# Attention's running totals: from one VectorE addition a unit to an identity product on TensorE and two copies on ScalarE

## The reference, cut to what matters

```python
h = (x @ W.T).reshape(n, H, D)                      # H = 8 heads of D = 32
alpha = einsum(h[src], a_src) + einsum(h[dst], a_dst)
enc = relu(edge_attr @ edge_W.T + edge_b).reshape(-1, H, D)
alpha = alpha + sum(enc * h[dst], axis=-1)
alpha = where(alpha >= 0, alpha, 0.2 * alpha)
amax = segment_max(alpha, dst)
ex = exp(alpha - amax[dst])
denom = segment_sum(ex, dst)
attn = ex / maximum(denom[dst], 1e-10)
out = segment_sum(h[src] * attn[..., None], dst)
```

## Time and profile before

| | us |
|---|---|
| median of 3 runs | 2576.47 |
| lowest, highest | 2573.31, 2578.95 |
| the profiled execution's own time | 2573.98 |
| its span, first to last instruction | 2572.2 |
| attention, first to last instruction (1429.5 to 2113.4) | 683.9 |
| of it, first group's sums to group 100's (1478.5 to 2079.2) | 600.7 |

### The profile page before, as it was taken

How to read it: one execution, slowest core, us unless ns; L and a number is a source line. 1 busy time by engine, 2 the same in 40 slices (tenths; PEclk the granted TensorE clock), 3 DMA queues, 4 the chain that set the end, 5 groups by cost and what they waited for, 6 DMA issues and landing times. The chain is left out here.

```text
span 2572.2 us, 42829 instructions
## 1 busy us (share of the span) xinstructions
PE 1882.3 (73%) x12059; PEld 1450.7 (56%) x12059; DVE 1646.2 (64%) x3381; ACT 839.1 (33%) x2217; POOL 1187.9 (46%) x1128
## 2 busy tenths in 40 slices
PE   3266666654299974799927777777777867978997
PEld 1245454543177753699925455555555642328997
DVE  7565656553187777665567499999999987022222
ACT  7333333322000011233316344444444433423332
POOL 0277777777400000355500577777777710004442
PEclk9687878777599996899968899999999998988999
DMA  3265555444588824222251455555555515101111
GB/s 81 77 202 186 197 179 179 169 165 164 185 296 292 294 104 151 91 71 73 69 173 37 147 148 145 142 146 145 147 144 144 144 56 211 37 1 50 51 53 30
DMA packets 198893, 345.71 MB, mean 134 GB/s; under 512 B 63569, under 2 KB 114738, under 8 KB 198287
## 3 DMA queue, kind: packets, MB, share of 16 engines
q1 hardware_dynamic: 145306, 196.20, 23.3%
q0 software_dynamic: 53088, 146.77, 19.0%
q10 hardware_dynamic: 274, 0.00, 0.0%
HBM read 222.74 MB, written 121.04 MB: 134 GB/s over the span
## 5 line engine op out<-in xcount | busy, mean ns | idle before, releaser
L1967 POOL DMA_INDIRECT att_rows<-hdram,top_ix x440 | 507.6, 1154 | 265.6 <-issue 133.2
L861 POOL DMA_INDIRECT mtab<-first_w,msgs_ix x280 | 276.7, 988 | 85.4 <-issue 80.8
L1163 POOL IOTA route_column<- 128x50 f32 (+1 forms) x2 | 0.3, 169 | 548.1 <-ACTq L1159 548.1
L1398 PE MATMUL exp_y<-exp_own,exp_ht 128*128 128x256 f32 x1032 | 239.0, 380 | 2.4 <-issue 2.4
L2048 PE MATMUL att_p_acc<-att_msg,att_hot 128*128 128x264 f32 x880 | 224.1, 399 | 21.1 <-DVE att_total L2220 13.3
L729 PE MATMUL msgs_p_m<-nodes_n,msgs_hott 128*128 x592 | 184.8, 466 | 46.3 <-issue 27.6
L2082 ACT ACTIVATE att_enc<-att_p_z 128x1024 f32<-128x1024 f32 x110 | 112.6, 1023 | 298.2 <-PE att_p_z L1988 298.2
L1398 PEld LDWEIGHTS exp_y<-exp_own,exp_ht 128*128 128x128 f32 x1032 | 188.7, 190 | 24.6 <-issue 3.1
L2048 PEld LDWEIGHTS att_p_acc<-att_msg,att_hot 128*128 128x128 f32 x880 | 161.8, 194 | 59.6 <-issue 32.7
L861 POOL DMA_INDIRECT mtab<-msgs_rw,msgs_ix x160 | 159.6, 998 | 69.8 <-issue 45.1
L627 DVE TENSOR_TENSOR first_w<-msgs_p_m,msgs_sorted 128x1024 f32<-128x1024 f32 x70 | 85.6, 1223 | 141.9 <-PE msgs_p_m L729 116.5
(11 more groups left out here) (403 smaller groups left out, 4003.0 us busy)
## 6 DMA issues: line engine op xcount, KB each, us to landing
first_w<-mtab SPq DMA_DIRECT2D x77, 520.0 KB, 4.6
etab<-msgs_et SPq DMA_DIRECT2D x110, 288.0 KB, 2.5
att_hz<-etab SPq DMA_DIRECT2D x110, 288.0 KB, 2.9
msgs_rw<-mtab SPq DMA_DIRECT2D x45, 520.0 KB, 4.7
first_w<-in_L_ffn_w SPq DMA_DIRECT2D x16, 512.0 KB, 4.6
ffn0x_w<-in_L_ffn_w SPq DMA_DIRECT2D x16, 512.0 KB
ffn_w<-in_L_ffn_Wd SPq DMA_DIRECT2D x8, 1024.0 KB, 10.7
att_rows<-hdram,top_ix POOLq DMA_INDIRECT x440
```

What stands on the lines that cost most here:

```text
L861: nc.gpsimd.indirect_dma_start(mtab, bass.IndirectOffsetOnAxis(ap=ix[:, g, q:q + 1], axis=0), rw[g % RS][:, q, :], None).then_inc(s_free[g ...
L1398: last = T.matmul(y[t % 2][:, 0:C], ht[t % 2][:, f, :], own2[:, f, :], start=(f == 0), stop=(f == FC - 1))
L1967: nc.gpsimd.indirect_dma_start(rows[:, g % RS, q, :], None, hdram, bass.IndirectOffsetOnAxis(ap=ix1[:, g, q:q + 1], axis=0)).then_inc(s_ro ...
```

## The change

TensorE now makes the whole total. Behind the two products of a unit it adds a third of the same width: the identity matrix times the tile `total[(u - 1) % TS]`, into the same bank, so that the bank then holds old total plus new sums. ScalarE reads the bank twice: once into the tile `total[u % TS]`, times `keep` of the next unit (a plain copy where the next unit begins a batch), and once into the bucket's place in `acc`. VectorE's `gathered` is gone; what stays there is one multiplication a batch by `fall` (`fallen`), on the tile that the next identity product reads. `keep_totals(s - 10)` at the head of ScalarE's step becomes `totals(s - 8)` at its end.

```diff
                     for r in range(UQ):
                         q = u % GU * UQ + r
                         last = T.matmul(p_acc[u % 2][:, 0:HW], hot[g % 2][:, q, :], msg[g % 2][:, q, :],
-                                        start=(r == 0), stop=(r == UQ - 1))
+                                        start=(r == 0), stop=(u == 0 and r == UQ - 1))
+                    if u and u % BU == 0:
+                        pe.wait_ge(s_fallen, u // BU)
+                    elif u:
+                        pe.wait_ge(s_total, u)
+                    if u:
+                        last = T.matmul(p_acc[u % 2][:, 0:HW], cst["ident"][:], total[(u - 1) % TS], start=False, stop=True)
                     last.then_inc(s_acc, 1)
...
-            def keep_totals(g):
+            def totals(g):
                 for u in range(g * GU, (g + 1) * GU):
                     b = act.value_load(gb[0:1, u:u + 1], min_val=0, max_val=NT - 1)
-                    act.wait_ge(s_add, u + 1)
+                    act.wait_ge(s_acc, u + 1)
+                    if u + 1 < NU and (u + 1) % BU:
+                        S.activation(total[u % TS], p_acc[u % 2][:, 0:HW], ACT.Copy, scale=keep[:, u + 1:u + 2]).then_inc(s_total, 1)
+                    elif u + 1 < NU:
+                        S.copy(total[u % TS], p_acc[u % 2][:, 0:HW]).then_inc(s_total, 1)
                     if u:
                         act.wait_ge(s_kept, u)
-                    S.copy(acc[:, bass.ds(b, 1), :].rearrange("p a c -> p (a c)"), total[u % TS][:]).then_inc(s_kept, 1)
+                    S.copy(acc[:, bass.ds(b, 1), :].rearrange("p a c -> p (a c)"), p_acc[u % 2][:, 0:HW]).then_inc(s_kept, 1)
...
-            def gathered(u):
...
+            def fallen(t):
+                to = total[(t * BU - 1) % TS].rearrange("p (h d) -> p h d", d=D + 1)
+                dve.wait_ge(s_fall, t + 1)
+                dve.wait_ge(s_total, t * BU)
+                V.tensor_tensor(to, to, bc(fall[t % 2][:], 2, D + 1), ALU.mult).then_inc(s_fallen, 1)
```

More of the change, by code:

```diff
@@ L1927, in attention @@
     (s_z, s_enc, s_h, s_prod, s_red, s_adst, s_al, s_line, s_chain, s_rb, s_back, s_backc, s_top, s_new, s_fall, s_edge,
-     s_dif, s_ex, s_msg, s_wide, s_acc, s_add, s_go, s_weight, s_kept) = (a.sem(m) for m in (
+     s_dif, s_ex, s_msg, s_wide, s_acc, s_total, s_go, s_weight, s_kept, s_fallen) = (a.sem(m) for m in (
          "z", "enc", "h", "prod", "red", "adst", "al", "line", "chain", "rb", "back", "backc", "top", "new", "fall", "edge",
-         "dif", "ex", "msg", "wide", "acc", "add", "go", "weight", "kept"))
+         "dif", "ex", "msg", "wide", "acc", "total", "go", "weight", "kept", "fallen"))
     s_rows, s_hz, s_seg = ([a.sem(f"{m}{s}") for s in range(k)] for m, k in (("rows", RS), ("hz", SE), ("seg", 2)))
@@ L2044, in sums @@
                     if u >= 2:
-                        pe.wait_ge(s_add, u - 1)
+                        pe.wait_ge(s_kept, u - 1)
                     for r in range(UQ):
@@ L2124, in _ @@
                 t, j = s // BG, s % BG
-                if 0 <= s - LAG - 3 < NUG:
-                    keep_totals(s - LAG - 3)
                 if s + 1 < NUG:
@@ L2138, in _ @@
                     widen(s - LAG)
+                if 0 <= s - LAG - 1 < NUG:
+                    totals(s - LAG - 1)
             act.wait_ge(s_kept, NU)
@@ L2208, in messages @@
                                 bc(ex[t % 2][:, j * G:(j + 1) * G, :], 3, D), ALU.mult).then_inc(s_msg, 1)
-            def gathered(u):
[L2211 to L2225, removed]
+            def fallen(t):
[3 more added lines that the diff above has]
+                V.tensor_tensor(to, to, bc(fall[t % 2][:], 2, D + 1), ALU.mult).then_inc(s_fallen, 1)
             same_windows()
             link(V.memset(tops[:, 0, :], -BIG))
-            link(V.memset(total[TS - 1][:], 0.0))
             for s in range(NUG + LAG + 3):
@@ L2239, in _ @@
                     differences(t - 1)
-                if 0 <= s - LAG - 2 < NUG:
-                    for u in range((s - LAG - 2) * GU, (s - LAG - 1) * GU):
-                        gathered(u)
+                if s > LAG + 1 and (s - LAG - 1) % BG == 0 and (s - LAG - 1) // BG < NB:
+                    fallen((s - LAG - 1) // BG)
                 if 0 <= s - LAG < NUG:
```

## The result

The changed kernel takes 2602.78 us (median of 3 runs, 2602.27 to 2606.14), the kernel before 2576.47. The profiled execution spans 2600.9 us, against 2572.2.

The account below looks back on a forecast made before the run. VectorE bounds the kernel before; afterwards TensorE's held sequencer sets the batch. Batches +30, low clock +3 and end +6 make +39 on the profiled 2573.98, 2613; with 2.5 us to the median, 2616, range 2598 to 2655.

Parts of the forecast that it names:

- What bounds it: Steady attention: VectorE sets the pace, busy 23.17 of 24 us; afterwards its share is about 0.77, TensorE's about 0.87.
- The scaled copy: ScalarE's activation from PSUM with a scale read from `keep`: taken as 0.48 us, range 0.39 to 0.60.
- The held sequencer: TensorE's second identity product waits until 2.15 us into the step; `offsets` registers and number loads are held behind it.
- The batch: Four attention steps of 6.04, 6.04, 6.15 and 6.89 us: 25.1 against 23.93, 30 us more over 25 batches.
- rival A: TensorE's sequencer passes the waiting product: a batch takes 23.1 us and the kernel 2561; chance 0.04.
- +3: Array time lost to TensorE's low clock, granted at 0.92 in 2000 to 2078, and dips elsewhere: 3 us more.
- The end: Stage's end, only sums left: groups every 2.9 us against 2.22; eight groups by 0.7 give 6 us more.
- C: ScalarE comes late to the first bank, its copy starting 0.5 us later each step: +50 us, 2666; chance 0.12.
- D: TensorE, busier, gets its full clock less often; at 0.92 throughout, 2 us a batch, again +50; chance 0.08.
- B: Double counting in the steps is 1.2 us a batch, so a batch stays at 23.9 us: 2576 + 6; chance 0.04.

Follow-up runs that it names:

- experiment 1: The changed kernel with the two bucket-number loads moved between the sums of a group's two units, one step further ahead: 2535.54 us, ratio 0.9851 to the kernel before.
- experiment 3: The changed kernel with the second unit's identity product reading the total of two units earlier, already done, so sums differ: 2534.25 us, ratio 0.9851.
- experiment 6: The changed kernel with ScalarE's two copies of a bank exchanged, the copy to `acc` first and the scaled one second: 2665.85 us, ratio 1.0354.
- experiment 2: The kernel before with only the bucket-number loads moved between the sums of a group's two units: 2571.97 us, ratio 0.9993.

## Why the prediction was right, point by point

- **What bounds it.** Right. VectorE's share fell to 0.79 (foreseen 0.77), and nothing came of the 3.9 us taken from it, because the path moved to TensorE's sequencer. TensorE's share is 0.82, not 0.87: it is busy for 20.6 us of a batch, where I had 18.3 + 3.6 = 21.9. The sum of the steps didn't use this number. Most of the 1.3 is in the timelines: before, each wait of the array let the last product ahead of it run out, 0.14 to 0.16 us that count as busy, and there were four more such waits a batch (0.6 us); and behind VectorE's `alphas` L2013 and L2006 took 0.99 us, where they take 0.56 now (0.4).
- **The scaled copy.** 0.481 us by the median of 110; foreseen 0.48. The pointer's 0.092 us, read from two lines of an earlier stage, held. The Trainium skill (ScalarE: Activation LUTs, What ACT_TABLE_LOAD costs) states about 93 ns for a pointer operand; the trace agrees: 0.481 against L2121's plain 0.379 is 0.102. The copy to `acc` is shorter than in the earlier trace rows, 0.373 against 0.412, now that it reads PSUM.
- **The held sequencer.** Right, and the step on which the sign rested. The registers start at 1711.2, within 0.1 us of the scaled copy's end, 2.2 us into the step (foreseen 2.15). Experiments 1 and 3 removed the two halves of this, the work behind and the wait ahead, and each brought 67 to 69 us. The Trainium skill's sentence on the wait queue (Perfetto Trace Analysis, Tensor Engine Instruction) would have given rival A's 2561. No run here agrees with it for a product whose wait isn't met.
- **The batch.** Plain steps 6.10 and 5.96 (foreseen 6.04), first 6.21 (6.15), second 6.82 (6.89): 25.09 against 25.1.
- **Before's own average.** Here 3 us were mis-sized. I took 30 us for 25 batches against 23.93; but before's average, with its low clock at the end, was 24.03, so it is 26.6. And I added 3 for the low clock: the clock stayed at 1.00 from 1500 to 2100, so nothing came. The term "+3" should have been -3. Before, it was granted at 0.92 in the last 78 us of the steady part; why this didn't recur isn't shown.
- **The end.** +5.2 us (foreseen +6). Where only sums are in the way, groups at the end follow every 2.67 to 3.06 us, against 2.22; I had 2.9. Two more, at the lower clock, take 4.2 and 4.4: from 2100 to 2145 it was granted at 0.92.
- **The 13 us between forecast and result.** 3.4 from the batches (30 against 26.6), 3 from the clock, 0.8 from the end, and 3 from what lies ahead of and behind the steady part and the end, which I had taken as unchanged and which scatters by a few us (the first sums start between 1476.3 and 1483.9 us in the traces of the chips where before takes 2573 to 2576). The last 2.5 are chance: the forecast was raised because the profiled execution of before lay 2.5 below its median, while that of the changed kernel is its median.
- **Rivals.** C fell: the scaled copy starts 0.04 us after its bank is closed. D fell with the clock at 1.00. The lower clock does come in every second batch of experiment 6, at 16 us in all, but TensorE is no busier there (0.80 of the time from group 0 to group 100, with some records missing, against 0.82), so that isn't D's mechanism. B and A fell with the batch's length.

What the forecast didn't say is that the change is one edit away from a gain. It had a rival in which the sequencer passes the wait, at 2561; the kernel that takes the numbers from behind the wait is at 2535. Its batch is 22.3 us where A had 23.1: the 0.30 us that stood ahead of L1988 in each step are gone as well, and GpSimd sets the pace.

## What to carry to other kernels

When work moves from a full engine to one with idle time, ask where on the new engine its input arrives, and what is queued behind. A product that waits holds its sequencer, so scalar loads and address arithmetic belong ahead of the last wait of a loop's body, or between two waits, and not at its end. An edit of this kind has to be tried together with the order around it: the same moved loads were worth nothing before the change (0.9993) and 67 us after it.

## What the runs showed of the hardware

- Loading a number into a register of TensorE's sequencer costs 0.65 us: 0.30 for the load, 0.15 for the arithmetic and 0.2 between them. With the array fed, two of these in a step cost nothing (experiments 1 and 2).
- TensorE's clock fell to its lower level (1.2 GHz) in twelve of 25 batches of experiment 6, shortly behind idle times of 1.10 to 1.23 us, and never in the changed kernel from 1500 to 2100, with 0.98 to 1.26 us in every step. The idle time just ahead doesn't decide it. A drop cost 1.4 us. With the numbers doubled, and 2.4 us of idle time in a step, the granted clock was 0.90 from 1700 to 2300.
- A timeline row that holds fewer products than its neighbours of the same line (x1 for x2) has lost a record, and the idle time printed ahead of it is too long by that product: 1.45 for 1.10 us in experiment 6.
- A low clock costs nothing where another engine bounds: 0.91 in experiment 2 left the batch at 23.9 us.
- A fetch issued by GpSimd takes 0.95 us alone, but one that starts while VectorE is in a long product with both inputs in SBUF ends some 0.83 us after that product, unless it started in the product's last 0.1 us. (Beside the bf16 product of the chain of maxima it is 0.77 to 0.79.) From the changed kernel:

```profile
1718.05 1.22 DVE L2216 TENSOR_TENSOR att_msg<-att_rows,att_ex 128x1024 f32<-128x1024 f32 x1 [0.27 <-PE att_p_acc L2055]
1718.57 1.54 POOL L1967 DMA_INDIRECT att_rows<-hdram,top_ix  x1 [0.30 <-issue]
...
1721.27 1.22 DVE L2164 TENSOR_TENSOR att_enc<-att_enc,att_p_h 128x1024 f32<-128x1024 f32 x1 [1.14 <-PE att_p_h L1997]
1721.66 0.95 POOL L1967 DMA_INDIRECT att_rows<-hdram,top_ix  x1 [0.30 <-issue]
```

  The second product reads PSUM for one input, and the fetch beside it isn't longer; 62 such fetches in experiment 1 average 0.95 us. Of the 51 us by which the fetches in experiment 1's 500 us exceed 0.95 each, 49 belong to those that started beside a product of the first kind. It is this that makes the mean fetch 1.09 us, and with it the bound of experiment 1.
